# A four-layer graph network on one core: the aggregate chunks are loaded from ScalarE's queue instead of SyncE's

## What is computed

```
x = layernorm(x + L0(x, node_vec1, edge_attr_16, edge_attr_4, src, dst, ...))
x = layernorm(x + L1(x, edge_attr_16, edge_attr_4, ..., edge_index))      # attention over the edges of a node
x = layernorm(x + L2(x, edge_attr_4, edge_attr_8, ..., edge_index))
x = layernorm(x + L3(x, node_vec1, edge_attr_4, edge_attr_8, src, dst, ...))

# the part per node, L2, where agg is the segment sum of the messages:
out   = agg @ W2 + x @ Wsc            # scalars (96) and vectors (32 x 3)
feats = [silu(out_s[:64]), out_v * silu(out_s[64:96])]
return x + feats
# L0: x @ Wsc * attr + alpha * agg     L1: x + agg
# L3: cos(angle) * (x @ Wsc) + sin(angle) * agg, the angle from agg and attr
```

## Time and profile before

| | us |
|---|---|
| median of 3 runs | 6270.43 |
| lowest and highest | 6266.55, 6278.46 |
| the profiled execution, its own time | 6268.0 |
| the span of the profile | 6266.2 |
| node stage of layer 0, about | 525 |
| node stage of layer 1, about | 290 |
| node stage of layer 2, about | 576 |
| node stage of layer 3, about | 720 |

### The profile page before, as it was taken

One profiled execution on the slowest core, in us unless ns is written; L12 is line 12 of the kernel. 1 busy time (PEld: TensorE's weight loads), 2 busy tenths in 40 slices (PEclk: granted clock), 3 DMA queues, 4 the chain that ended last, 5 costly groups with the idle time before them and its releaser, 6 DMA issues. The chain is left out here.

```text
span 6266.2 us, 75219 instructions
## 1 busy us (share of the span) xinstructions
PE 4745.8 (76%) x14104; PEld 2187.4 (35%) x14104; DVE 3728.6 (60%) x10260; ACT 2222.0 (35%) x5204; POOL 3319.1 (53%) x4175
## 2 busy tenths in 40 slices
PE   0799966659999999999992068886666788865555
PEld 0233345533333333333330023334545333334444
DVE  2566645547888888787877744544555455544444
ACT  0232335542222222222224643333555433333333
POOL 0466657764443344443423456764333566667776
PEclk9999977777777777777775579987787899976666
DMA  8222246651222222222217932223555222234444
GB/s 341 75 69 68 67 126 185 188 159 48 52 51 58 51 52 52 53 54 51 54 42 219 339 111 65 66 65 109 181 179 183 79 67 68 66 107 133 138 134 124
DMA packets 545372, 677.81 MB, mean 108 GB/s; under 512 B 57166, under 2 KB 387106, under 8 KB 545052
## 3 DMA queue, kind: packets, MB, share of 16 engines
q1 hardware_dynamic: 451888, 496.01, 26.9%
q0 software_dynamic: 86400, 142.71, 8.3%
q10 hardware_dynamic: 7020, 38.40, 1.5%
HBM read 449.48 MB, written 245.49 MB: 111 GB/s over the span
## 5 line engine op out<-in xcount | busy, mean ns | idle before, releaser
L491 POOL DMA_INDIRECT aggregates<-agg_out,scatter_index x600 | 616.9, 1028 | 415.5 <-issue 245.4
L1185 PE MATMUL psum<-identity,x_chunk 128*128 128x128 f32 x1176 | 259.1, 361 | 671.5 <-issue 627.5
L1242 ACT ACTIVATE y_chunk<-residual,ln_minus_mean_rstd,ln_rstd 128x160 f32<-128x160 f32 x1568 | 685.6, 508 | 207.2 <-DMA x_layer<-y_chunk 105.4
L1263 POOL TENSOR_TENSOR ln_rstd<-ln_var_eps,minus_half 128x4 f32<-128x4 f32 x392 | 398.4, 1016 | 665.1 <-DVE ln_minus_mean L1381 572.8
L1196 PE MATMUL psum<-self_weights,x_chunk_T 128*128 128x160 f32 (+1 forms) x2352 | 630.4, 436 | 25.8 <-ACT x_chunk_T L1221 23.5
L746 POOL TENSOR_TENSOR edge_ln_rstd<-edge_ln_var,minus_half 128x16 f32<-128x16 f32 x50 | 146.9, 2938 | 851.4 <-DVE edge_ln_var L1002 851.4
L1196 PEld LDWEIGHTS psum<-self_weights,x_chunk_T 128*128 128x128 f32 x2352 | 545.6, 284 | 70.1 <-ACT x_chunk_T L1221 29.2
L567 PE MATMUL psum<-identity,scaled_x 128*128 128x128 f32 x600 | 145.4, 281 | 501.8 <-ACT scaled_x L513 479.3
L850 PE MATMUL psum<-rbf_times_sh,weights_layer 64*96 64x512 f32 (+1 forms) x600 | 513.1, 1039 | 2.1 <-DVE leaky_and_tanh L1007 1.3
L474 POOL DMA_INDIRECT gathered<-x_layer,gather_index x400 | 402.7, 1007 | 177.0 <-issue 120.2
L1185 PEld LDWEIGHTS psum<-identity,x_chunk 128*128 128x128 f32 x1176 | 169.9, 181 | 770.9 <-issue 770.9
(11 more groups left out here) (202 smaller groups left out, 10711.3 us busy)
## 6 DMA issues: line engine op xcount, KB each, us to landing
x_layer<-y_chunk SPq DMA_DIRECT2D x294, 320.0 KB, 4.6
x_chunk<-x_layer SPq DMA_DIRECT2D x294, 320.0 KB, 3.6
agg_chunk<-aggregates SPq DMA_DIRECT2D x196, 320.0 KB, 5.7
sh_rows<-in_sh_big SPq DMA_DIRECT2D x50, 768.0 KB, 5.8
agg_chunk<-aggregates SPq DMA_DIRECT2D x98, 384.0 KB, 4.3
aggregates<-agg_out ACTq DMA_DIRECT2D x48, 768.0 KB
x_chunk<-in_x SPq DMA_DIRECT2D x98, 322.0 KB, 2.9
agg_chunk<-aggregates SPq DMA_DIRECT2D x98, 322.0 KB, 4.3
```

Of the source, the lines that this page charges most:

```text
L491: eng.indirect_dma_start(agg_table[:, :], bass.IndirectOffsetOnAxis(idx_last[:, q, b:b + 1], 0), agg_out[:, q, b, :], None, bounds_check=N ...
L1185: eng.transpose(psum[:, 2 * q, b * 128:b * 128 + 128], x_in[:, buf, b, 0:128], ident[:, :])
L1242: op = eng.activation(y_out[:, buf, b, :], res[:, buf, b, :], ACT.Identity, bias=shift[:, buf, b:b + 1], scale=rstd[:, buf, b:b + 1])
L1263: eng.tensor_tensor(rstd[:, buf, :], var_eps[:, q, :], minus_half[:, 0:T], ALU.pow)\
```

## The change

The instruction that loads a chunk's aggregates moves from SP's stream into ACT's. On ACT it stands at the head of step s, ahead of all the work of that step, together with the wait for the residual of chunk s-4 that protects the buffer. SP keeps the load of x and the store. Both loads still raise the same semaphore, so nothing changes for those who wait for them. ACT also waits for the end of the scatters, once per node stage. The wait for `transposed` stays on SP alone.

```
--- before.py
+++ after.py
@@ -1148,8 +1148,6 @@  node_sync
                     else:
                         eng.dma_start(x_in[:, par, :, 0:D], x_table[l][rows, :].rearrange("(p j) c -> p j c", j=T))\
                            .then_inc(sem, 16)
-                    eng.dma_start(agg_in[:, par, :, 0:agg_cols[l]],
-                                  agg_table[rows, 0:agg_cols[l]].rearrange("(p j) c -> p j c", j=T)).then_inc(sem, 16)
                 lag = summed(l) + 3
@@ -1206,8 +1204,18 @@
         def node_scalar(eng, l):
             S = NODE[l]
+            scattered(eng, l)
 
             def step(s, par):
+                if live(s, 0, NC):
+                    c = s
+                    held(eng, c - 3, S["res"])
+                    apart(eng)
+                    wait(eng, S["res"], c - 3)
+                    rows = bass.ds(chunk(c), GE)
+                    eng.dma_start(agg_in[:, par, :, 0:agg_cols[l]],
+                                  agg_table[rows, 0:agg_cols[l]].rearrange("(p j) c -> p j c", j=T))\
+                       .then_inc(S[f"load{par}"], 16)
                 if l != 1 and live(s, TURN - 1, NC):
```

## The result

| | us |
|---|---|
| before, median of 4 runs (6257.03 to 6278.46) | 6268.49 |
| changed, median of 4 runs (6412.54 to 6421.55) | 6413.43 |
| ratio, with its 95% interval | 1.0235 [1.0215, 1.0254] |
| predicted | 6381 (6300 to 6460) |

A forecast was written before the change was run, and what follows sets the result against it. Latency was taken to bound layer 2, DMA engines layer 1, and chains through POOL and DVE layers 0 and 3. +108 (layer 2's circle) +3 (its start) +0 elsewhere gave +111 us, 6381 us; range 6300 to 6460.

The forecast's parts named there:

- The circle of one period in layer 2: Layer 2: copy, linear map, `node_mid`, statistics, residual, ACT's wait, issue and copies form one circle each period; +108 us.
- Its length: Layer 2's forecast period: 5.90 + 0.21 + 0.47 + 0.15 + 0.22 = 6.95 us per chunk, against 5.84 us.
- from the start of the large copy to the end of the residual: Layer 2: first term of the period, 5.90 us as the mean of 5.90, 5.10 and 6.69 us.
- the larger risk: Layer 2: TensorE idles longer in each period, so its clock is expected rather lower; a risk upward in time.
- The forecast for the upper level throughout: Layer 2 with TensorE at its upper clock level throughout: 5.10 + 1.05 = 6.15 us per chunk, +30 us.
- ACT's issue: Layer 2: issuing the load on ACT takes 0.47 us, ends 0.39 and 1.0 us.
- rival A: Issue holds all of ACT for about 1.0 us: layer 2 +49 us, layer 1 +20 us, total 6450 us; chance 0.14.
- Layers 0 and 3: 0: Residual lags three chunks, the circle has two periods, and slack takes the later copies; 0 us.
- Layer 1: 0, with -5 as the lower end: DMA engines already full at 111.9%, so a second queue has nothing to fill; 0 us, ends -5 and +40 us.
- over 350 GB/s would show me wrong: Layer 1: sign against the forecast if its GB/s, 331 before, rose over 350.
- The start of the stage: +3 us: Layer 2's start: two first loads wait behind ACT's first copies; +3 us, 0 to +8.
- case of the lower level: Layer 2 with TensorE at its lower clock level: 6.69 + 1.05 = 7.74 us per chunk, +184 us.

The follow-up runs named there:

- e1: Against the kernel before: ACT issues the aggregates' load in layer 2 alone, SP in layers 0, 1 and 3; 6416.77 us, ratio 1.0233.
- e2: Against the kernel before: ACT issues the aggregates' load in layers 0, 1 and 3 alone, SP in layer 2; 6264.22 us, ratio 0.9997.
- e3: Kernel before, SP issuing both loads, with only the wait for the residual added at the head of ACT's step in layer 2; 6359.42 us.
- e6: Changed kernel with ACT's wait and aggregates' load moved behind the copies and the silu in layer 2; 6251.39 us.
- e12: Changed kernel with 12 extra transposes per chunk on TensorE in layer 2, which nothing reads; 6276.92 us.
- e4: Kernel before with a further small transfer issued at the head of ACT's step in layer 2, without a wait for the residual; 6261.69 us.
- e9: Changed kernel with a semaphore of their own for the aggregates' loads; 6428.02 us.
- e7: Kernel before with a semaphore of their own for the aggregates' loads, so ACT's small copy and TensorE's transposes wait for x alone; 6187.08 us, ratio 0.9884.
- e10: Changed kernel with own semaphores for the aggregates' loads and, in layer 2, ACT's wait and load behind the silu; 6265.81 us, ratio 0.9994.

## Why the prediction was right, and where it was off

- **The circle of one period in layer 2.** Right: named in the prediction with its links, seen in the trace of the changed kernel, located by e1 and e2, closed by the wait alone in e3, opened by another place in e6.
- **Its length.** 6.95 us forecast for the steady part, 7.57 us measured there (7.42 us over the whole stage). The term that was mis-sized is the first one, from the start of the large copy to the end of the residual: 5.90 us as the mean of three cases of before, where the changed kernel has 6.61 us on the mean from 4360 to 4860 (6.75 us in the period shown). That is near the slow case of the three, 6.69 us, in nearly every period. I had the clock down as the larger risk and upward, but took a mean over the levels of the kernel before. In the changed kernel TensorE waits 2.35 us on the mean for the small copy, and none of the 66 maps from 4360 to 4860 runs at the upper level throughout: the first eight matmuls take 2.1 to 2.9 us, where e12 has 1.56 us. The forecast for the upper level throughout, 6.15 us, can be held against e12, with 5.94 us in the same stretch.
- **ACT's issue.** 0.47 us taken, 0.34 us measured; with all that lies between the end of the residual and the small copy 0.83 us taken, 0.74 us measured on the mean. The wide upper end (1.0 us, rival A) was not needed. Rival A's premise, that an issue holds the whole engine, doesn't hold in layer 1, where activations run beside it (last section).
- **Layers 0 and 3: 0.** Right, 1.2 and 0.6 us. ACT's small copy does start later behind the residual, in layer 0 1.00 us after its end where it was 0.12 us, and the slack takes it. In layer 3 it starts some 3 us later against the residual, as forecast (0.9 us behind its end at 6003.92, where at 5806.80 it stood 2.3 us ahead of it), and that slack takes it too. Layer 0 in the changed kernel:

```profile
1099.73 0.83 DVE L1366 TENSOR_TENSOR residual<-node_mid,agg_chunk 128x640 f32<-128x640 f32 x1 [2.31 <-POOL agg_chunk L1321]
...
1101.56 0.31 ACT L1223 ACTIVATE x_last_columns<-x_chunk 128x128 f32<-128x128 f32 x1 [2.77 <-DVE residual L1366]
...
1105.02 0.82 DVE L1366 TENSOR_TENSOR residual<-node_mid,agg_chunk 128x640 f32<-128x640 f32 x1 [2.40 <-POOL agg_chunk L1321]
```

- **Layer 1: 0, with -5 as the lower end.** Wrong, though small. It came to -4.8 us in the trace of the changed kernel, and to about -8 us on the mean of the seven traces on either side (see e1 and e2). The step that failed is that a second queue has nothing to fill because the packets' times sum to 111.9% of the engines: in the changed kernel that share stayed near 1.1 (1.08 for 1.10), and yet the same work was done in less time. A share above 1 did not mean here that nothing was left to gain. I had written that over 350 GB/s would show me wrong: the stage has 336 against 331, but its middle, from 3400 to 3500, has 351 here and 355 in e2, where it was 337. SP's store issues fell to 0.42 us in the median, not to 0.33. Whether the gain comes from the second queue's transfers or from the issue that SP no longer has to make was not tried.
- **The start of the stage: +3 us.** Wrong in sign: from the first load to the first residual it is 13.8 us (4288.3 to 4302.1), where it was 16.3 us (4308.0 to 4324.3). e1 has 14.1 us and e3 and e4 15.7 us, so this is not one odd trace; why it is so stays open.
- **The sum.** 111 us forecast, 145 us measured. Layer 2 alone cost 163 us, 52 us more than the 111 us: 46 us by the circle (7.42 for 6.95 us), 12 us because the kernel before has 5.72 and not 5.84 us over the whole stage, less some 6 us at the start. Layer 1 and the edge stages, 5 and 15 us shorter in these two executions, hid 20 us of that. That the time lies so near the forecast is luck in this part; the measured time is within the range, between the forecast and its upper end, and layer 2's 163 us lie between the forecast and its case of the lower level, 184 us.

## What to carry to other kernels

A DMA issue brings its buffer's wait with it. On SP, which computes nothing, this wait cost nothing here; at the head of a compute engine's step it ties that engine to whoever frees the buffer. Count, for every awaited result, how many steps lie between it and the work behind the wait: with two periods in the circle (layers 0 and 3) the move was free, with one (layer 2) it lengthened the stage by 28%. Then ask what the new idle time does to TensorE's clock: here that decided the size of the loss. Before moving a load, look whether those who wait for it read it at all: giving each load its own semaphore gained 1.2% in the kernel before, more than any place of the issue, and nothing in the changed one.

## What was not expected of the hardware

**ACT issues a DMA while it still computes.** In layer 1 of the changed kernel the issue stands in the program behind the four instructions of the normalization, and yet it runs beside them, between the start of the first and the end of the last:

```profile
3452.48 0.52 ACT L1250 ACTIVATE y_chunk<-residual,ln_minus_mean_rstd,ln_rstd 128x160 f32<-128x160 f32 x1 [1.14 <-DMA x_layer<-y_chunk]
...
3452.76 0.55 ACTq L1216 DMA_DIRECT2D agg_chunk<-aggregates  x1
...
3452.90 1.34 ACT L1250 ACTIVATE y_chunk<-residual,ln_minus_mean_rstd,ln_rstd 128x160 f32<-128x160 f32 x3
```

The four follow one another without a pause, so the 0.55 us cost nothing there. Behind the wait in layer 2 ACT has nothing left to compute, and there the issue is paid for.

**With a second queue it is the transfers of the first one that land later.** In layer 1 of the changed kernel the later of the two landings comes 10.1 us after its issue in the median, where the aggregates had 6.5 us before (and were issued 0.75 us behind x). The profile puts the later landing down to the aggregates, but both loads raise one semaphore there, so it can't tell them apart. e9 has a semaphore for each. In its layer 1, from 3370 to 3600, it is x, on SP's queue, that lands last:

```profile
x_chunk<-x_layer SPq DMA_DIRECT2D x83, 320.0 KB, 10.0
agg_chunk<-aggregates ACTq DMA_DIRECT2D x83, 320.0 KB, 7.5
```

In e7, with own semaphores and one queue, x takes 6.3 us in layer 1. SP's stores, too, take 9.4 us to land in the changed kernel, where they took 6.5 us. Layer 1's stage is shorter all the same. Where a load's landing is in the circle, as that of x is in layer 2 of e7 and e10, a second queue may cost what it seems to save.

**The clock can cost more than the wait that lowers it.** In layer 2 the changed kernel has a period of 7.42 us; 12 transposes per chunk that nothing needs bring it to 5.86 us.
